# Routed expert blocks sent to node rows by numbers that travel with the rows, instead of being fetched back by slot

## The reference

```python
def _bank_residual(x2, Wr, br, W1, b1, W2, b2):      # called twice, with the bank "sp" and the bank "fq"
    probs = jax.nn.softmax(x2 @ Wr + br, axis=-1)     # 8 experts
    expert = jnp.argmax(probs, axis=-1)
    gate = jnp.take_along_axis(probs, expert[:, None], axis=-1)[:, 0]
    ...                                               # rows are put into their expert's slots
    h = jax.nn.gelu(buf @ W1[e] + b1[e])              # 512 -> 128, per expert
    out = h @ W2[e] + b2[e]                           # 128 -> 512
    return out[slot] * gate[:, None]
y = gelu(x2 @ Ws1 + bs1) @ Ws2 + bs2 + _bank_residual(sp) + _bank_residual(fq)
return x1 + y
```

## Time and profile before

| | us |
|---|---|
| median of 3 runs (510.04 to 511.16) | 510.18 |
| the profiled execution's own time | 506.99 |
| its span (first to last instruction) | 505.2 |
| PE busy | 455.2 (90%) |
| DVE / ACT / POOL busy | 215.1 / 167.5 / 183.8 |
| last block's result is out of PSUM (L1579) | 481.67 |
| last DVE instruction ends | 502.48 |

### The profile page before, as it was taken

The page is one execution under the profiler, slowest core; times in us unless marked ns, Lnnn a source line. Parts: engine busy times, 40 slices in busy tenths (PEclk is TensorE's granted clock), DMA queues, the critical chain, the costliest instruction groups (busy, mean ns, idle before and its releaser), DMA issues.

```text
span 505.2 us, 7437 instructions
## 1 busy us (share of the span) xinstructions
PE 455.2 (90%) x2602; PEld 319.0 (63%) x2602; DVE 215.1 (43%) x518; ACT 167.5 (33%) x365; POOL 183.8 (36%) x210
## 2 busy tenths in 40 slices
PE   2799799989999999898999999999999999996990
PEld 2354346768665755575667787877777787764670
DVE  5779981222352727353311002431013758732244
ACT  2799673222310021911222013431035530232310
POOL 3101200074410722297054762406116419920252
PEclk9999999999999999999999999999999999999996
DMA  5999999969999969975702723030003357769566
GB/s 123 384 424 420 424 424 361 331 231 342 394 384 417 355 213 401 377 272 186 272 1 72 219 112 138 3 106 2 3 22 84 123 211 214 262 217 369 177 179 193
DMA packets 38788, 119.27 MB, mean 236 GB/s; under 512 B 7050, under 2 KB 7111, under 8 KB 30302
## 3 DMA queue, kind: packets, MB, share of 16 engines
q1 hardware_dynamic: 35390, 114.91, 61.6%
q0 software_dynamic: 3360, 3.86, 3.1%
HBM read 103.92 MB, written 14.82 MB: 235 GB/s over the span
## 4 chain that ended last, share of the span: by engine, by line
PE 76%; issue 6%; DVE 5%; DMA 3%; ACT 3%; POOL 3%; SPq 2%; DVEq 1%; POOLq 0%
PE ps L1621 14%; PE ps L1623 13%; PE ps L1622 13%; PE ps L1645 10%; PE ps L1980 9%; PE ps L1706 5%; PE ps L1825 2%; PE ps L2102 2%; PE ps L2112 2%; ACT h_tmp L1362 1%; DMA got<-y_dram,slot_u 1%; DMA y_dram<-ybuf 1%; PE ps L1629 1%; POOL piece_lo L742 1%; DMA x_raw<-x_dram 1%
## 5 line engine op out<-in xcount | busy, mean ns | idle before, releaser
L1645 PE MATMUL ps<-ring,sel_att 128*32 128x512 f32 x512 | 66.0, 602 | 6.2 <-DMA ring<-in_L_gnn_basis_dram 2.6
L1621 PE MATMUL ps<-piece_hi,ht_hi 128*125 128x512 f32 x140 | 56.1, 401 | 0.8 <-PE ps L1623 0.6
L1623 PE MATMUL ps<-piece_hi,ht_lo 128*125 128x512 f32 x140 | 55.1, 394 | 0.0
L1622 PE MATMUL ps<-piece_lo,ht_hi 128*125 128x512 f32 x140 | 55.1, 394 | 0.0
L1099 DVE SCALAR_TENSOR_TENSOR u_lo<-ps,gates,u_hi 125x512 fp32r<-125x512 f32 x20 | 15.0, 751 | 94.1 <-ACT u_hi L1508 94.1
L741 POOL CAST piece_hi<-piece_raw 128x512 fp32r<-128x512 f32 x28 | 19.8, 707 | 91.3 <-issue 53.7
L742 POOL TENSOR_TENSOR piece_lo<-piece_raw,piece_hi 128x512 fp32r<-128x512 f32 x28 | 37.8, 1351 | 13.3 <-issue 11.2
L949 DVE TENSOR_SCALAR oh_n<-iota_n,keys 125x626 f16<-125x626 f16 x100 | 37.8, 378 | 8.1 <-PE ps L1706 6.0
L1980 PE MATMUL ps<-u_hi,cf 125*125 125x512 f32 x100 | 39.9, 398 | 1.3 <-PE ps L1623 1.3
L1980 PE MATMUL ps<-u_lo,cf 125*125 125x512 f32 x100 | 39.4, 394 | 0.0
L1706 PE MATMUL ps<-oh_n,oh_m 125*128 125x313 f16 x200 | 31.4, 314 | 4.1 <-DVE oh_m L950 4.1
(11 more groups left out here) (333 smaller groups left out, 927.3 us busy)
## 6 DMA issues: line engine op xcount, KB each, us to landing
ring<-in_L_gnn_basis_dram SPq DMA_DIRECT2D x64, 1024.0 KB, 11.7
w_home<-in_L_ffn_W_sp_dram SPq DMA_DIRECT2D x27, 256.0 KB, 5.9
y_dram<-ybuf SPq DMA_DIRECT2D x18, 256.0 KB, 5.2
rel_dram<-stag SPq DMA_DIRECT2D x16, 256.0 KB, 8.3
w_raw<-rel_dram SPq DMA_DIRECT2D x8, 512.0 KB, 6.8
w_fq<-in_L_ffn_W_fq_dram SPq DMA_DIRECT2D x2, 2048.0 KB, 10.6
piece_raw<-in_L_mix_Wkqv_dram SPq DMA_DIRECT2D x3, 1024.0 KB, 10.7
x_dram<-stag SPq DMA_DIRECT2D x1, 3072.0 KB
```

Source lines behind the costliest of these rows:

```text
L1621: pe.matmul(target, a_hi, b_hi, start=first, stop=False, skip_group_check=skip)
L1622: pe.matmul(target, a_hi, b_lo, start=False, stop=False, skip_group_check=skip)
L1623: return pe.matmul(target, a_lo, b_hi, start=False, stop=last, skip_group_check=skip)
L1645: last = pe.matmul(ps[32 * c:32 * c + 32, rel_bank(ch), :], sel_att[:, ch // CHUNKS, g].rearrange("p r q -> p (r q)"), ring[slot][:, c * D ...
```

## The change

Each row carries its node number: `x_dram` and `x_raw` rows are 520 words instead of 512, and the eight extra words hold the node number (for empty slots a number from 625 up, which SP writes first). POOL takes the number of every row of a block (`take_ids`) and, when the block's second layer is out of PSUM, scatters the block's 128 rows straight to their node rows of `y_dram[1]` (`scatter_block`, 12 indirect DMAs). When all have landed SP reads `y_dram[1]` plainly, 125 rows to a DMA. Bank 0 is still gathered by slot; two of its five gathers go behind scatters 4 and 6, three behind the last. Further: PE's tiles are run two to a round at first, `load_rows` go ahead of the stores, SP's twelve stores of bank 1 are gone, bank 1 has 12 result buffers of its own and bank 0 three, `move_w1` for blocks 4 to 11 goes from POOL to DVE, `load_rows(0)` no longer waits for the last unit split, and DVE's last adds are in another order.

```diff
-XRAWS, XTS, W1S, HSS, YBUFS = 5, 4, 4, 5, 7
+XRAWS, XTS, W1S, HSS, YBUFS = 5, 4, 4, 5, (3, NB_FQ)
+DX = D + 8
+GATHER_BEHIND = (4, 6)
+TILES_AT = {2: (0, 1), 3: (2, 3), 4: (4,), 5: (5, 6)}
...
 # SP
+            sp.dma_start(x_rows[:, :, D:DX], empty_id[:].bitcast(F32)).then_inc(zeroed, 16)
...
                 if i == 0:
                     sp.wait_ge(scattered, SCATTERED)
+                if i == 3:
                     sp.wait_ge(unit_lo, len(UNITS))
                 if i >= XRAWS:
                     sp.wait_ge(hT_t, 3 * NT + i - XRAWS + 1)
+                    sp.wait_ge(ids_ready, IDS_SEEN + i - XRAWS + 1)
...
-            for i in range(2, NB_FQ + 2):
-                if i + XRAWS - 2 < NB_FQ:
-                    load_rows(i + XRAWS - 2)
-                if i - 2 < NY:
-                    store_block(sp, 0, i - 2)
-                store_block(sp, 1, i - 2)
-                if i + 2 in (4, 5, 6):
-                    load_tile(i + 2)
+            for i in range(2, 6):
+                if i == 2:
+                    for r in range(XRAWS, XRAWS + 3):
+                        load_rows(r)
+                load_rows(i + XRAWS + 1)
+                for j in TILES_AT[i]:
+                    store_block(sp, 0, j)
+                for j in {2: (4, 5), 3: (6,)}.get(i, ()):
+                    load_tile(j)
+            for i in range(NY - YBUFS[0], NY):
+                sp.wait_ge(*y_landed(0, i))
+            sp.wait_ge(y_scattered, 16 * NB_FQ)
+            for t in range(NT):
+                sp.dma_start(got[1][:, t, :], y_dram[1][t * TP:(t + 1) * TP, :]).then_inc(got_fq[t], 16)
...
 # POOL
+            def take_ids(i):
+                pool.wait_ge(raw_in[i % XRAWS], ...)
+                pool.tensor_copy(slot_id[:, i:i + 1], x_raw_id[i % XRAWS]).then_inc(ids_ready, 1)
+            def scatter_block(i):
+                pool.wait_ge(ids_ready, IDS_SEEN + i + 1)
+                pool.wait_ge(*y_done(1, i))
+                pool.indirect_dma_start(y_dram[1], bass.IndirectOffsetOnAxis(ap=slot_id[:, i:i + 1], axis=0),
+                                        y_buf(1, i), None).then_inc(y_scattered, 16)
+            def gather_rows(t):
+                if t == 0:
+                    for i in range(NY - YBUFS[0], NY):
+                        pool.wait_ge(*y_landed(0, i))
+                pool.indirect_dma_start(got[0][:, t, :], None, y_dram[0], ...).then_inc(got_sp[t], 16)
...
-            for i in range(W1S, NB_FQ):
-                move_w1(i)
-            gather(0)
-            gather(1)
+            for i in range(NB_FQ):
+                if i == 0:
+                    for r in range(XRAWS):
+                        take_ids(r)
+                elif i + XRAWS - 1 < NB_FQ:
+                    take_ids(i + XRAWS - 1)
+                scatter_block(i)
+                if i in GATHER_BEHIND:
+                    gather_rows(GATHER_BEHIND.index(i))
+            for t in range(len(GATHER_BEHIND), NT):
+                gather_rows(t)
...
 # ACT and DVE, before a result is copied out (was: one wait on the buffer's store)
+                if b == 0 and i >= YBUFS[0]:
+                    dve.wait_ge(*y_landed(b, i - YBUFS[0]))
...
 # DVE, rounds i = 2 to 11
-                if i - 2 < NY:
-                    take_block(0, i - 2)
+                for j in TILES_AT.get(i, ()):
+                    take_block(0, j)
                 take_block(1, i - 2)
+                if i + 2 < NB_FQ:
+                    move_w1(i + 2)
...
 # DVE, tail: add_shared is the old L1286, add_second the old L1291, add_first the old L1281
+            for t in range(NT + 2):
+                if t < NT:
+                    add_shared(t)
+                if 0 <= t - 1 < NT:
+                    add_second(t - 1)
+                if t >= 2:
+                    add_first(t - 2)
...
 # PE, rounds i = 2 to 11
-                if i - 2 < NY:
-                    block_tile(i - 2)
+                for j in TILES_AT.get(i, ()):
+                    block_tile(j)
                 block_second(i - 2)
```

More of the change, by code:

```diff
@@ L279, in gnn_mix_ffn @@
         HOME = [0, 1, 2, 3, 0, 1, 2]
-        got = [place(f"got{b}", [TP, NT, D], F32, a) for b, a in enumerate((r_raw, r_u + KB512))]
-        x_raw = [place(f"x_raw{i}", [128, D], F32, r_raw + i * 2048) for i in range(XRAWS)]
+        got = [place(f"got{b}", [TP, NT, D], F32, a) for b, a in enumerate((r_split, r_u + KB512))]
+        x_raw = [place(f"x_raw{i}", [128, DX], F32, r_raw + i * DX * 4) for i in range(XRAWS)]
+        x_raw_id = [a[:, D:D + 1].bitcast(U32) for a in x_raw]
         xs_t = [place(f"xs_t{i}", [128, KT, SB_FQ], F32, r_split + 16384 + i * 2048) for i in range(XTS)]
@@ L317, in gnn_mix_ffn @@
         w1_fq_in, W1_FQ_SEEN, w1_moved = rel_back[0], 32, sem("w1_moved")
-        y_out, Y_SEEN = basis_in[0:7], [16 * (3 + (10 if i < 4 else 0)) for i in range(7)]
+        y_out, Y_SEEN, y_scattered = (basis_in[0:3],), ([16 * 13] * 3,), sem("y_scattered")
         w2_fq_in, W2_FQ_SEEN = rel_back[1], 32
         k_hi_done = sem("k_hi_done")
-        zeroed, ZEROED = rows_in, 16 * 12
+        zeroed, ZEROED = rows_in, 16 * 13
         scattered, SCATTERED = sem("scattered"), 16 * NT
@@ L475, in y_buf, with y_landed @@
         def y_buf(b, i):
[L476 to L488, removed]
+            return ybuf[b][i % YBUFS[b]][0:SB_FQ if b else y_rows(i), :]
+        Y_HOME_FREE = {4: 3, 8: 4}
+        def y_landed(b, i):
+            s = i % YBUFS[b]
+            return y_out[b][s], Y_SEEN[b][s] + 16 * (i // YBUFS[b] + 1)
         def store_block(queue, b, i):
@@ L826, in move_w1 @@
                                  ).then_inc(w1_moved, 1)
[L828 to L837, removed]
+            def take_ids(i):
+                pool.wait_ge(raw_in[i % XRAWS], 16 * ((4 if i % XRAWS < 2 else 0) + len(UNITS) // RAWS + i // XRAWS + 1))
+                pool.tensor_copy(slot_id[:, i:i + 1], x_raw_id[i % XRAWS]).then_inc(ids_ready, 1)
[8 more added lines that the diff above has]
+                        pool.wait_ge(*y_landed(0, i))
+                pool.indirect_dma_start(got[0][:, t, :], None, y_dram[0],
+                                        bass.IndirectOffsetOnAxis(ap=slot_u[:, t, 0:1], axis=0)).then_inc(got_sp[t], 16)
             pool.wait_ge(smalls_in, 16 * 10)
@@ L1251, in take_block, with move_w1 @@
                 dve.wait_ge(o_mm, ORDER_OF[b, i] + 1)
-                if ORDER_OF[b, i] >= YBUFS:
-                    dve.wait_ge(*y_buf_free(b, i))
+                if b == 0 and i >= YBUFS[0]:
+                    dve.wait_ge(*y_landed(b, i - YBUFS[0]))
+                if b == 1 and i >= 4:
+                    dve.wait_ge(o_mm, ORDER_OF[0, Y_HOME_FREE[i // 4 * 4]] + 1)
                 n = SB_FQ if b else y_rows(i)
-                dve.tensor_copy(ybuf[y_buf(b, i)][0:n, :], ps[0:n, turn_bank("o", (b, i)), :]).then_inc(y_dve, 1)
+                dve.tensor_copy(y_buf(b, i), ps[0:n, turn_bank("o", (b, i)), :]).then_inc(y_dve, 1)
+            def move_w1(i):
+                if i == W1S:
+                    dve.wait_ge(w1_fq_in, W1_FQ_SEEN + 16)
+                dve.wait_ge(h_mm, W_AT + i - W1S + 1)
+                _, (expert,) = nc.values_load_multi_w_load_instructions(
+                    block_ei[0:1, NB + i:NB + i + 1], engines=[mybir.EngineType.DVE], min_val=0, max_val=E - 1,
+                    skip_runtime_bounds_check_because="VectorE limits each number to 0 .. E - 1 where it makes it")
+                dve.tensor_copy(w1_home[i % W1S][:].rearrange("p t f -> p (t f)"),
+                                w1_fq[:].rearrange("p e t f -> p e (t f)")[:, bass.ds(expert, 1), :].rearrange("p e n -> p (e n)")
+                                ).then_inc(w1_moved_dve, 1)
             for m in range(3, 2 * NT):
@@ L2098, in block_first @@
                 pe.wait_ge(*rows_turned(i))
-                pe.wait_ge(w1_moved, i + 1)
+                if i < W1S:
+                    pe.wait_ge(w1_moved, i + 1)
+                else:
+                    pe.wait_ge(w1_moved_dve, i - W1S + 1)
                 pe.wait_ge(*bank_free("w", i))
```

72 lines of the change are left out of this document (40 added, 32 removed).

## The result

The changed kernel takes 511.5 us (median of 20 runs, 509.0 to 515.3) against 510.1 for the kernel before (20 runs, 506.2 to 515.1). The ratio is 1.0046, with a 95% interval of 1.0024 to 1.0069: about 2.3 us slower (the interval is 1.2 to 3.5 us; the two medians differ by 1.4). The forecast was 512.5, which is +2.3.

A forecast was written before the change was run, and what follows sets the result against it. Bound: a chain of waits, 20.8 us from last result to last add. Loop 0, then scatter start 3.2, landing 4.7, reads 13.1 and adds 2.1 make 23.1: 510.18 + 2.3 = 512.5 us, range 507.8 to 516.5.

The forecast's parts named there:

- main case: Whole kernel: loop gain lost to weight waits, reads queued on five engines; 511 to 515 us, chance 0.45.
- Early parts: Ahead of the block loop: number fills, SP's number write, longer rows and earlier `load_rows(0)` cost 0, bound 0.5.
- Loop: PE's block loop: 3.9 of `x_raw` waits and 0.9 of restarts go, `W2` stalls of 2.2 and 2.8 come; net 0.
- `move_w1` on DVE: Block loop: eight weight copies on DVE, 0.32 to 0.69 each, fit in its slack; 0, bound +1.
- rival 3: POOL's queue: each scatter pays its wait anew, 518.8 us, chance 0.10; weak form: DVE copies and POOL exclude each other, 1.5.
- POOL, last scatter at 484.9: POOL's queue behind the loop: DMAs 1.5 apart start the last scatter 2.2 late, 3.2 after the last result.
- Landing: From the last scatter's start to its rows being in DRAM: 4.7 us, bounds 3.9 and 6.54.
- Reads: SP's five plain 125-row reads, one after another on five DMA engines, 2.0 each: 13.1 us, last landing at 502.7.
- Adds: DVE's tail after the last read: one second and two first adds, 2.1 us, last add at 504.8.
- Behind the last add: End of the kernel: what follows the last add, the last output store, is the same in both kernels.
- Rival 1: SP's plain reads spread over all DMA engines: last add at 501.2, 508.9 us, chance 0.25.
- Rival 2: Block loop: the `W2` loads come in time, everything 4 earlier, last add at 500.8, 508.5 us; chance 0.15.

The follow-up runs named there:

- e4: Changed kernel with one tile per PE round (rounds 2 to 8), one gather behind scatter 8 and four behind the last; ratio to the kernel before 0.997.
- e7: Kernel before with only SP's row loads moved ahead of its stores; ratio to the kernel before 0.991.
- e6: Changed kernel with each of the five plain reads cut into 64 and 61 rows; 533.5 us in one run.
- e1: Changed kernel with each of the five plain reads cut into 112 and 13 rows; ratio to the kernel before 0.997.
- e10: Changed kernel without gathers 2 to 4 of bank 0, tiles 2 to 4 adding tile 1's gathered rows instead; 511.6 us in one run.
- e5: Changed kernel with the edits of e4 and e1 together; ratio to the kernel before 0.987.
- e8: e5 with all five gathers of bank 0 behind the last scatter, none between scatters; ratio to the kernel before 0.988.
- e13: e8 run a second time, unchanged; ratio to the kernel before 0.985.

## Why the prediction was right

The time and the sign came out by the main case. Four terms in it were off, by 1.3 to 2.3 each, and nearly cancelled.

- **Early parts, 0.** Nothing shows them: the difference from the first turn on is as large as the result. The start of the loop spreads over 5 us between profiles, so a cost of some tenths ahead of it stays open.
- **Loop: gains 4 to 5, loses as much.** The mechanism held: no wait on `x_raw`, and 1.95 and 3.25 on `w_home` where 2.2 and 2.8 were forecast. e4 and e7 show the cause: 38.0 with the same early row loads and no two tiles in a round. Mis-sized was the end: last result 44.1 after the first turn, not 42.8. I had counted 0.9 of slow restarts as gone with the old waits; the new wait of 3.25 brought its own, at a granted clock of 0.50 in 471 to 473: of the 6.1 over e4, 5.2 are waits and 0.9 is the rest. The 0.9 that goes with the old waits was right too: e7's loop is 4.8 shorter for 3.9 of waits. The size of this term also moves from profile to profile. The four kernels with packed tiles have 44.1, 44.6, 45.4 and 47.1 (changed, e6, e1, e10), the seven profiles with early row loads and tiles apart 38.0 each; so the 1.3 by which this profile missed the forecast is the least of the four. In each of the four the granted clock is at 0.50 for some 4 to 7 us around the second wait on weights.
- **`move_w1` on DVE, 0.** Right: eight copies, 0.42 in the median and 0.61 the longest, and no engine waited for them. The lock between DVE's and POOL's SBUF work that I had weighed as a weak form of rival 3, at up to 1.5, can be no more than the 0.2 by which the longest copy stands out.
- **POOL, last scatter at 484.9 (489.5 with the shift).** 489.20. Its parts were smaller, 0.97 instead of 1.21 for one scatter and 0.19 instead of 0.35 for a number copy, which took back the 1.3 by which the results were late. Nor did the queue hold to the end: POOL had caught up by the third scatter from the last, and the last one starts 1.6 behind the last result, where 3.2 was forecast.
- **Landing 4.7: mis-sized.** The last scatter starts at 489.20, and SP goes on at 491.96: 2.76, below my lower end of 3.9. I had added an issue of 1.21 to a 2.7 that already begins with an issue; that this is the reason is argued, not shown.
- **Reads, 13.0.** 15.3 from first issue to last landing (507.26). One after another on five engines was right: 0.32 at 127 GB/s, starts 2.0 to 2.7 apart (forecast 2.0). Without the gathers they take 12.5 (e10), near the 12.0 that I had without sharing. What I put at 1.0, the sharing with the gathers, is 2.8. Most of it falls on the first read, which took 6.3, not 4.0.
- **Adds, 2.1.** 2.05.
- **Behind the last add, "the same in both".** 3.3 against 2.7 and 2.8: 0.5 to 0.6 that the sum left out.

Loop +1.3, scatter start -1.6, landing -1.9 and reads +2.3 make 0.1. The forecast of the last add, 504.8, is 509.4 with the shift; measured were 509.31. This agreement to 0.1 is luck, and it holds for one profile. Of the bounds, landing fell 1.1 below its own, and the reads were as long as their upper end.

Rival 1 (reads over all engines) is dead by the shares and by e6. Rival 2 (weights in time) is false for this order, and true as soon as the tiles stand apart (e4). Rival 3 (POOL's waits paid anew) is dead: the last scatters come 1.27 apart.

So the change holds one gain and two losses, and each was made or undone in a run of its own (e4 moves the gathers too). SP's early row loads are worth 0.9% alone (e7). Packing the tiles costs PE 6.1 in the loop (e4 against the changed kernel), and up to 9.1 in the other packed profiles. The uncut reads cost 2.4 in the tail (e1), and more when the rest is faster: 4.7 from e4 to e5. Scatter and plain reads in place of store and gather, freed of both, end at 57.0 to 58.1 after the first turn against 58.9 for e7, and the intervals of their ratios (0.985 to 0.988, and 0.991) overlap: that the new way of bank 1 is better at all is not shown. The best versions are e5 and e8, 1.2 to 1.5% faster than the kernel before and, from the ratios, 1.7 to 2.0% faster than the changed one.

## What to carry to other kernels

Cost a transfer by how many DMA engines its row count gives it, not by its bytes: a busy share of a third while such a transfer is alone says so, and 112 + 13 rows instead of 125 mends it. When loads are moved earlier, look for what is packed closer in the same edit, as its loads can be late next. And where one edit makes results earlier, look at what is queued on the in-order engine that hands them on: of the 6.1 that e4 gained in the loop, 3.1 stayed on POOL and in the reads.

## What was not expected of the hardware

- An indirect store of 128 rows (256 KB) takes POOL 0.97, an indirect load of 125 rows 1.21, and SP can go on 2.8 after the last store's start (3.1 in e5 and 3.4 in e4, where a gather stands among the scatters).
- A transfer on one engine: 61 rows of 2 KB in 5.2 to 5.4, share 0.07 at 27 GB/s; on five, 127 to 131 GB/s.
- How long SP takes to issue depends on what its transfers meet: five reads of 125 rows took it 2.0 without gathers beside them (e10) and 3.7 with them, ten of 112 and 13 rows 4.4 (e1), ten of 64 and 61 rows, queued on few engines, 19.5 (e6). What stands behind them on SP waits as well, here the output stores.
- Gathers and cut reads together fill the DMA engines at about 250 GB/s (254 at a share of 0.98, 226 at 1.03), where loads and stores of blocks fill them at 406.
- PE's granted clock halves for 3 to 7 us (1.2 instead of 2.4 GHz) in some executions although PE is busy without a gap, and in another of the same kernel it does not (e8 and e13). The cause stays open.
